# A 3x3 quantised convolution and a gated attention-free layer on one core: second layer in two TensorE visits a quarter instead of four

## The reference

```
# layer 0: x = x + L0(_gn(x))
v  = round(clip(x * in_factor, -1, 1) * 127) / 127 * 0.6, H and W swapped, padded by 1
fv = patches + 0.1 * patches ** 3                        # 3x3 patches of v
g  = g_pos - g_neg                                       # 3 planes of 128x128x3x3 weights
outs[i] = einsum('bctfyx,ocyx->btfo', fv, g[i])          # 3 convolutions
mem = adc(outs[2]) + adc(outs[0]) * 4 + adc(outs[1]) * 2 + adc(outs[2])
L0  = mem * out_factor + bias
# layer 1: x = x + L1(_gn(x)), with z = _gn(x) as 128 x 4096 per image
q, k, v = Wq z, Wk z, Wv z                               # 64 x 4096 each
num = exp(B) (exp(k) * v);  den = exp(B) exp(k)
L1  = Wm (q * num / den)
```

## Time and profile before

| | us |
|---|---|
| median of 3 runs | 1563.71 |
| the profiled execution | 1562.54 |
| its span in the trace | 1560.5 |
| PE busy | 1454.3 (93%) |
| DVE busy | 1393.6 (89%) |
| ACT busy | 1155.7 (74%) |
| POOL busy | 503.7 (32%) |

### The profile page before, as it was taken

How to read it: one execution, slowest core, us unless ns; L and a number is a source line. 1 busy time by engine, 2 the same in 40 slices (tenths; PEclk the granted TensorE clock), 3 DMA queues, 4 the chain that set the end, 5 groups by cost and what they waited for, 6 DMA issues and landing times.

```text
span 1560.5 us, 22719 instructions
## 1 busy us (share of the span) xinstructions
PE 1454.3 (93%) x7792; PEld 622.2 (40%) x7792; DVE 1393.6 (89%) x2182; ACT 1155.7 (74%) x1501; POOL 503.7 (32%) x506
## 2 busy tenths in 40 slices
PE   2599999999999999999999999999999999999985
PEld 1354434344443434444343443434344443434332
DVE  5869898998989899898989989898998989899767
ACT  4447778786877878787787878778786877875463
POOL 3111333232433333243333323333332433333312
PEclk9799999999999999999999999999999999999997
DMA  5011012313222231322223132222313222221222
GB/s 203 1 54 30 26 28 50 113 28 108 55 63 73 55 108 28 108 55 70 67 54 109 28 109 57 57 80 53 110 28 108 55 58 78 55 55 28 68 68 81
DMA packets 29173, 103.80 MB, mean 67 GB/s; under 512 B 4032, under 2 KB 4224, under 8 KB 29056
## 3 DMA queue, kind: packets, MB, share of 16 engines
q1 hardware_dynamic: 20416, 70.86, 12.3%
q0 software_dynamic: 8640, 31.46, 10.6%
HBM read 37.29 MB, written 33.55 MB: 45 GB/s over the span
## 4 chain that ended last, share of the span: by engine, by line
PE 74%; DVE 18%; issue 5%; POOL 1%; ACT 1%; DMA 1%; DVEq 0%; SPq 0%; POOLq 0%; ACTq 0%
PE A L486 14%; PE A L488 12%; PE A L487 12%; PE L L546 7%; PE B L486 7%; PE B L488 7%; PE B L487 7%; PE L L590 4%; PE L L577 3%; DVE duo L1068 1%; DVE uall L1150 1%; DVE A L1120 1%; DVE duo L1117 1%; DVE uall L1123 1%; DVE q L1040 1%
## 5 line engine op out<-in xcount | busy, mean ns | idle before, releaser
L486 PE MATMUL A<-T,WH 128*128 128x504 f16 (+1 forms) x1152 | 438.9, 381 | 1.0 <-ACT uall L780 1.0
L488 PE MATMUL A<-T,WL 128*128 128x504 f16 (+1 forms) x1152 | 437.3, 380 | 0.0
L487 PE MATMUL A<-T,WH 128*128 128x504 f16 (+1 forms) x1152 | 437.3, 380 | 0.0
L1436 POOL TENSOR_TENSOR T<-t,T 128x512 f16<-128x512 f32 x192 | 244.5, 1298 | 407.5 <-ACT T L702 407.5
L745 ACT ACTIVATE junk<-xr,shift 128x1024 f16<-128x1024 f32 x244 | 280.1, 1148 | 7.3 <-DVE xr L1153 0.7
L1410 POOL TENSOR_TENSOR zl<-z,zh 128x512 f16<-128x512 f32 x120 | 150.8, 1276 | 397.7 <-ACT zh L813 396.7
L486 PE MATMUL B<-T,WH 128*128 128x504 f16 (+1 forms) x576 | 221.4, 384 | 25.9 <-POOL T L1436 16.3
L488 PE MATMUL B<-T,WL 128*128 128x504 f16 (+1 forms) x576 | 220.7, 383 | 0.9 <-issue 0.9
L487 PE MATMUL B<-T,WH 128*128 128x504 f16 (+1 forms) x576 | 220.7, 383 | 0.0
L486 PEld LDWEIGHTS A<-T,WH 128*128 128x128 f16 x1152 | 115.1, 100 | 194.0 <-issue 81.3
L488 PEld LDWEIGHTS A<-T,WL 128*128 128x128 f16 x1152 | 112.7, 98 | 136.2
(11 more groups left out here) (174 smaller groups left out, 2462.5 us busy)
## 6 DMA issues: line engine op xcount, KB each, us to landing
xr<-in_x_dram SPq DMA_DIRECT2D x64, 512.0 KB, 5.8
out_dram<-xr SPq DMA_DIRECT2D x64, 512.0 KB, 2.7
xr<-shared POOLq DMA_DIRECT2D x60, 512.0 KB, 4.6
xr<-in_L_conv_g_pos_dram SPq DMA_DIRECT2D x3, 576.0 KB, 9.4
xr<-in_L_conv_g_neg_dram SPq DMA_DIRECT2D x3, 576.0 KB, 11.8
xr<-in_L_conv_Wm_dram SPq DMA_DIRECT2D x2, 32.0 KB, 9.2
xr<-in_L_conv_Wq_dram SPq DMA_DIRECT2D x1, 32.0 KB, 11.3
xr<-in_L_conv_Wk_dram SPq DMA_DIRECT2D x1, 32.0 KB, 11.1
```

What stands on the lines that cost most here:

```text
L486: nc.tensor.matmul(to, wh, th, start=fresh and y == 1, stop=False, skip_group_check=True)
L487: nc.tensor.matmul(to, wh, tl, start=False, stop=False, skip_group_check=True)
L488: done = nc.tensor.matmul(to, wl, th, start=False, stop=y == 2, skip_group_check=True)
L1436: last = nc.gpsimd.tensor_tensor(low, t32[:, pair, :, :, :].rearrange("p t e w -> p (t e w)"), high, ALU.subtract)
```

## The change

The four visits of a quarter become two. The first does the keys and values of quarter k and, right after them, the mix of quarter k-1; it waits for `o_ready` of k-1 first. The second does the queries and then the sums of quarter k. Queries and mix now write `low_pair`, the pair that the convolution's taps 2 and 4 use, so PE waits for `m2_copied` before such a visit, and the convolution's next step waits for `q_copied` or `evicted` (`others_read`, `second_read`). ACT gets one more instruction a quarter, `copy_queries`, a copy of the queries to SBUF behind `guess`. DVE keeps four instructions after the sums, now all in `ratio`: the numerator is first multiplied by the queries. The mix is cut into 8 matmuls of 64x64 weights and 256 columns, where it was 2 of 64x128 and 512. Each quarter's slots stand in tables (`KV_PE` and so on; numbers from 36 up mean the following phase); `TAIL` holds those of image 14. The slot tuples of the first layer are changed as well. In the head, the scale of x comes before the second weight difference on POOL, the third difference waits for `sums_made` 2, and the low rows of group 1 of image 0 are made by DVE (`head_rows_low`) instead of POOL. The diff, without blank lines:

```diff
-L2_PE = (1, 3, 6, 7)
-L2_ACT = (1, 3, 6, 8)
-L2_DVE = (2, 5, 6)
-L2_POOL = (6, 8)
-X_STATS = (1, 3, 4, 6)
-X_SPREAD = 7
-X_GROUP = 9
-X_MOMENTS = 9
-COMBINE = (21, 0)
-DOUBLE = (12, 33)
-RESIDUAL = (25, 7)
-BIAS = (17, 31)
-X1_STATS = (28, 30, 9, 13)
-X1_SPREAD = 13
+KV_PE = (21, 32, 39, 45)
+SUMS_PE = (22, 33, 40, 46)
+KV_ACT = (21, 32, 39, 45)
+MIX_ACT = (32, 40, 45, 57)
+SUMS_ACT = (23, 34, 41, 45)
+Z_ACT = (18, 25, 35, 41)
+KV_DVE = (22, 33, 40, 46)
+SUMS_DVE = (24, 35, 42, 49)
+Z_POOL = (18, 25, 35, 42)
+ADD_POOL = (35, 42, 49, 59)
+TAIL = {"KV_PE": (20, 26, 32, 36), "SUMS_PE": (22, 28, 34, 38), "MIX_PE": (26, 32, 36, 39),
+        "KV_ACT": (20, 26, 32, 36), "SUMS_ACT": (22, 28, 34, 43), "MIX_ACT": (26, 32, 36, 46), "Z_ACT": (18, 23, 29, 35),
+        "KV_DVE": (21, 27, 33, 36), "SUMS_DVE": (23, 29, 35, 44), "Z_POOL": (18, 23, 29, 35), "ADD_POOL": (27, 33, 37, 48)}
+X_STATS = (0, 2, 4, 6)
+X_SPREAD = 9
+X_GROUP = 14
+X_MOMENTS = 15
+COMBINE = (20, 0)
+DOUBLE = (17, 35)
+RESIDUAL = (23, 8)
+BIAS = (17, 32)
+X1_STATS = (26, 31, 8, 9)
+X1_SPREAD = 12
 X1_GROUP = 15
-LOW = (28, 33, 7, 11)
+LOW = (28, 33, 8, 11)
 X1_MOMENTS = 15
-LEVEL = (17, 19, 21, 24)
-QUANTISE = (18, 20, 23, 26)
-SQUARE = (19, 22, 24, 26)
-CUBIC = (21, 22, 27, 29)
-TRANSFORM = (26, 31, 2, 13)
-HIGH = (27, 32, 6, 14)
+LEVEL = (17, 19, 20, 24)
+QUANTISE = (18, 20, 21, 25)
+SQUARE = (19, 21, 24, 26)
+CUBIC = (20, 22, 27, 33)
+TRANSFORM = (26, 29, 3, 11)
+HIGH = (30, 32, 6, 14)
...
+        q32 = pieces[3]
...
+        STEADY = {"KV_PE": KV_PE, "SUMS_PE": SUMS_PE, "MIX_PE": KV_PE[1:] + (KV_PE[0] + SLOTS,),
+                  "KV_ACT": KV_ACT, "SUMS_ACT": SUMS_ACT, "MIX_ACT": MIX_ACT, "Z_ACT": Z_ACT,
+                  "KV_DVE": KV_DVE, "SUMS_DVE": SUMS_DVE, "Z_POOL": Z_POOL, "ADD_POOL": ADD_POOL}
...
+        def second(name, p, slot, images):
+            prev2, prev = images[:2]
+            last = B - 1 if isinstance(p, int) and p >= B - 1 else None
+            if prev2:
+                table = TAIL if last and p - 2 == B - 2 else STEADY
+                for k, at in enumerate(table[name]):
+                    if at == slot + SLOTS:
+                        return p - 2, 2, k
+            if prev and (images[2] or not last):
+                table = TAIL if last and p - 1 == B - 2 else STEADY
+                for k, at in enumerate(table[name]):
+                    if at == slot:
+                        return p - 1, 3, k
+            return None
...
+            def others_read(p, slots, images):
+                prev2, prev, cur, nxt = images
+                for slot in slots:
+                    if slot == X_GROUP and nxt:
+                        pe.wait_ge(gvar[0], nth(p + 1, 1, 0))
+                    if slot == X1_GROUP and prev:
+                        pe.wait_ge(gvar[1], nth(p - 1, 1, 0))
+                second_read(p, slots, images)
+            def second_read(p, slots, images):
+                for slot in slots:
+                    at = second("MIX_PE", p, slot, images)
+                    if at:
+                        pe.wait_ge(evicted, nth(at[0], NG, at[2]))
+                    at = second("SUMS_PE", p, slot, images)
+                    if at:
+                        pe.wait_ge(q_copied, nth(at[0], NG, at[2]))
...
-                    if n == X_GROUP // 6 + 1 and nxt:
-                        pe.wait_ge(gvar[0], nth(p + 1, 1, 0))
-                    if n == X1_GROUP // 6 + 1 and prev:
-                        pe.wait_ge(gvar[1], nth(p - 1, 1, 0))
+                    if n:
+                        others_read(p, range(6 * n - 6, 6 * n), images)
+                    elif prev:
+                        earlier = (not (isinstance(p, int) and p <= 2), prev2, True, True)
+                        others_read(p - 1, range(SLOTS - 6, SLOTS), earlier)
...
             def keys_values(image, k, w):
                 pe.wait_ge(zh_ready, nth(image, NG, k))
-                if not w and (k or not (isinstance(image, int) and image == 0)):
-
-                    pe.wait_ge(evicted, nth(image, NG, k - 1))
...
-            def queries(image, k, w):
-                pe.wait_ge(ratio_ready, nth(image, NG, k))
-                project(banks[w][0], 0, w, crossed=True).then_inc(q_ready, 1)
-            def mix(image, k, w):
-                pe.wait_ge(o_ready, nth(image, NG, k))
-                for h in range(2):
-                    half = slice(h * IC, (h + 1) * IC)
-                    last = nc.tensor.matmul(banks[w][h], wmf[half, :], rec[w][half, :], start=True, stop=True)
+            def queries():
+                project(low_pair[:, 0, :], 0, 0, crossed=True).then_inc(q_ready, 1)
+            def last_queries(k):
+                pe.wait_ge(last_ratio, k + 1)
+                project(banks[k][0], 0, k, crossed=True).then_inc(q_ready, 1)
+            def mix(w, out):
+                for part in range(2):
+                    at = slice(part * QUART, (part + 1) * QUART)
+                    for r in range(2):
+                        rows = slice(r * IC, (r + 1) * IC)
+                        for c in range(2):
+                            cols = slice(c * IC, (c + 1) * IC)
+                            last = nc.tensor.matmul(out[r][cols, at], wmf[rows, cols], rec[w][rows, at],
+                                                    start=True, stop=True)
                 last.then_inc(mix_ready, 1)
-            def second_layer(image, c):
-                k, at = divmod(c, CYCLE)
-                if at == L2_PE[0]:
-                    keys_values(image, k, 0)
-                if at == L2_PE[1]:
-                    numerator_denominator(image, k, 0)
-                if at == L2_PE[2]:
-                    queries(image, k, 0)
-                if at == L2_PE[3]:
-                    mix(image, k, 0)
+            def second_layer(p, slot, images):
+                n, place = divmod(slot, 6)
+                values, mixed, summed_up = (second(name, p, slot, images) for name in ("KV_PE", "MIX_PE", "SUMS_PE"))
+                if mixed or summed_up:
+                    assert not images[2] or 2 <= place < 5
+                    if images[2]:
+                        pe.wait_ge(m2_copied, nth(p, STEPS, n))
+                        others_read(p, range(6 * n, slot), images)
+                    elif slot == 0:
+                        pe.wait_ge(m2_copied, nth(p - 1, STEPS, STEPS - 1))
+                        others_read(p - 1, range(SLOTS - 6, SLOTS), (True, True, True, False))
+                    else:
+                        others_read(p, range(slot), images)
+                    if X_GROUP == slot and images[3]:
+                        pe.wait_ge(gvar[0], nth(p + 1, 1, 0))
+                    if X1_GROUP == slot and images[1]:
+                        pe.wait_ge(gvar[1], nth(p - 1, 1, 0))
+                if mixed:
+                    pe.wait_ge(o_ready, nth(mixed[0], NG, mixed[2]))
+                if values:
+                    keys_values(values[0], values[2], 0)
+                if mixed:
+                    mix(0, (low_pair[:, 0, :], low_pair[:, 1, :]))
+                if summed_up:
+                    queries()
+                    numerator_denominator(summed_up[0], summed_up[2], 0)
...
-                    if slot == 2 and not cur:
+                    if slot == 1 and not cur:
...
+            def copy_queries(image, k):
+                act.wait_ge(q_ready, nth(image, NG, k))
+                nc.scalar.copy(q32, low_pair[:, 0, :]).then_inc(q_copied, 1)
...
-                                     last_pair[:, :, :].rearrange("p c (r n) -> p c r n", r=2), ACT.Identity,
+                                     low_pair[:, :, :].rearrange("p c (r n) -> p c r n", r=2), ACT.Identity,
...
+            def second_layer(p, m, slot, images):
+
+                at = second("KV_ACT", p, slot, images)
+                if at:
+                    exponent(at[0], at[2], 0)
+                at = second("MIX_ACT", p, slot, images)
+                if at:
+                    evict(at[0], at[2])
+                at = second("SUMS_ACT", p, slot, images)
+                if at:
+                    guess(at[0], at[2], 0)
+                    copy_queries(at[0], at[2])
+                at = second("Z_ACT", p, slot, images)
+                if at:
+                    z_split(at[0], (m + at[1]) % RING, at[2])
...
+            def head_rows_low(g):
+                for pair in range(3):
+                    dve.wait_ge(th_ready, NP * g + pair + 1)
+                    high, low = (T[:, part, pair, g * TILES:(g + 1) * TILES, :, :]
+                                 .rearrange("p t e w -> p (t e w)") for part in range(2))
+                    last = nc.vector.tensor_tensor(low, t32[:, pair, :, :, :].rearrange("p t e w -> p (t e w)"),
+                                                   high, ALU.subtract)
+                last.then_inc(tl_ready, 1)
...
             def ratio(image, k, w):
+                dve.wait_ge(q_copied, nth(image, NG, k))
```

(55 more changed lines are left out.)

80 lines of the change are left out of this document (35 added, 45 removed).

## The result

The changed kernel takes 1546.22 us (median of 4 runs, 1544.50 to 1546.89) against 1563.28 (4 runs, 1562.73 to 1565.27): ratio 0.9889 [0.9877, 0.9901], 17.1 us less. Forecast were 1533 and a range of 1515 to 1556. Sign and range hold; the gain is little more than half of what was forecast.

The account below looks back on a forecast made before the run. PE was taken to bound the steady part. Fewer visits 15.6, the ratio's wait 22.5, new waits -15.4, head 6.5 and tail 1.8 made 31.0 us less: 1533, range 1515 to 1556.

Parts of the forecast that it names:

- Fewer visits: PE: each join saves 0.11 us, the mix's new shape 0.04; 1.04 us an image, 15.6 in all (bounds 2.4 to 22.2).
- Rival (C): PE: the shape change inside a joined visit costs 0.11 us, leaving 2.4 of 15.6 us; 1546, chance 0.05.
- (d): Ratio before keys, eviction before queries (0.8 us ahead at best), POOL's low rows, ACT's extra copy: no new wait.
- (c): DVE's weighted values of quarter 1 (slot 33) come about 0.2 us late for PE's sums.
- (b): ACT's m2 copy at first visits comes late for PE: 0.35 us at slot 9, about 0.25 at slot 32.
- (a): ACT's queries' copy at second visits, slots 22, 40, 46: PE stalls about 0.1 us each, 0.3 an image.
- (A): Waits move to where PE and ACT meet in `low_pair`, 2.4 us an image; 12.8 less, 1551, chance 0.13.
- (B): Slower: queries' copy 1.25 us late at three second visits, 4.55 us new waits an image; 1581, chance 0.10.
- (D): DVE becomes the bound; contention with POOL adds 1 us to its run, 14 us come back; 1547, chance 0.10.
- The signs: Image 88.6 to 89.8 us; over 1 us wait at slots 22, 40 or 46 proves (B), L577 wait on DVE's values (D).
- The head: Before the first convolution matmul: PE starts at about 42.2 instead of 49.55 us; 6.5 us gained (bounds 2.5 and 8).
- The tail: Last phases: 5.9 us of waits go, 0.4 and 3.7 are lost; 1.8 us gained (bounds -4 and +6).

Follow-up runs that it names:

- the last run: Changed kernel plus the edits for statistics order, sums at slot 34, doubling at slot 33, queries' copy ahead of Ln and Exp, and image 14's later mix: 1521.63 us.
- the run with fewer low rows: Changed kernel with two of POOL's three low-row subtractions of group 2 left out from the third image on: 1534.98 us.
- The statistics run: Changed kernel with ACT's last two statistics pairs and quarter 3's Ln, Exp and copy one slot later, so the eviction comes ahead: 1532.29 us.
- The tail run: Changed kernel with image 14's last mix behind the group sums of image 15, its eviction, ratio and addition moved with it: 1545.58 us.

## Why the prediction was right or wrong

- **Fewer visits: right, in mechanism and size.** Forecast 2.44 and 1.79 us for the joined visits, measured 2.44 and 1.80; an image without waits is 90.21 - 2.1 = 88.1, as forecast, and 88.46 with 0.3 of waits in the last run. The Trainium skill ("TensorEngine Tiling (Array Packing)", section Tiling Modes, Key Properties) says that changing the tiling mode drains TensorE, and the trace agrees: every change of shape shows 0.31 us between starts instead of 0.22, at the entry to a visit (722.79 to 723.10), in its middle (724.21 to 724.52) and at its end (725.22 to 725.54). Two visits apart have four such changes and a joined visit three. One of them was already in each piece's own time, because the prediction counted that to the start of the next matmul; so the change in the middle is there, and the price of a join, one change less, holds. Rival (C), a further 0.11 us in each joined visit, is out.
- **The ratio's wait goes: right.** No row of it is left in the steady part.
- **(d), taken at nothing: this is the term that was wrong.** The prediction says "`evicted` before the queries of the next slot: 0.8 us ahead at best" and took it at nothing, although it added that "a shift of 1 us uncovers" it. It measured 1.05 us an image, 14.7 us in 14; the three other terms together came out as they were forecast, 1.08 against 1.1. That agreement is partly luck: (c) came out larger, (a) and (b) smaller. The walk through ACT's list used undisturbed durations; the residual that the statistics wait for was 3.30 us long and not 2.35, and L1225 ahead of it 1.99 and not 1.23. That is 1.7 us, against 0.8 of slack (1.9 with the clipping ahead of both, L1222, at 0.91 instead of 0.69, which leaves 1.1); the run with fewer low rows took 0.95 of it away, and that left 0.10 of the wait. The statistics run ended it too, by the order alone. The prediction had a row of such a stretch, 3.52 against 1.22 us, and used it for the head only; with it the term would have been an interval, 0 to about 1 us, and not nothing.
- **(c), the weighted values: right mechanism, size off.** 0.2 forecast, 0.58 measured. DVE's run from the values of one quarter to the next took 28.8 us instead of 28.5; it also started a little late, behind a quantisation.
- **(b), the copy of m2: about half.** Slot 32 as forecast (0.25, measured 0.32); at slot 9, where 0.35 was forecast, 0.03 to 0.1.
- **(a), the copy of the queries: less** than forecast (0.3): 0.18 an image.
- **The rivals.** (A), "the new meeting point of PE and ACT in `low_pair`", named this mechanism with 2.4 us an image and 1551. The result, 2.1 us an image and 1546, is nearer to it than to the forecast of 1.1 and 1533, and the 0.13 that it got was too little for a walk with three meetings within 0.4 us. (B) did not happen: the copy was late by 0.06 at each of its three places, not 1.25. (D) named contention of POOL with DVE and its size, 1 us an image, but made DVE the bound; it acted through ACT, and in the last run PE is busy for 88.19 of 88.46 us and DVE for 84.88. (C) and (D) name 1546 and 1547, the time that was measured, by mechanisms that the trace does not show; that is chance.
- **The signs were too loose.** A wait of more than 1 us at slot 46 "would prove B", and a wait of the sums on DVE's values D. Both came: the first matmul at slot 46 waits up to 1.3 us, the sums 0.58 an image. But the first waits for the eviction and not for the queries' copy, and the second stayed at half a microsecond. A sign has to name the instruction that is waited for, and the size.
- **The head: nearly right.** First convolution matmul at 41.71 us (forecast 42.2), 7.84 earlier. 5.8 us of it are left at the group sums (forecast 6.5), because 2.0 us are lost on the way and not 0.7; of the waits for the weights on that way one is shown below (L1034, 3.73 us). Timeline of the head, against the earlier trace rows: the transform's first instruction is back at 1.22, as forecast, but POOL's second difference now lies beside the sums of plane 0, and one of these (L1018) takes 3.12 us, where it takes 0.84 later, with POOL idle:

```profile
16.83 3.15 POOL L1460 TENSOR_TENSOR xr<-xr 128x1152 f32<-128x1152 f32 x1 [0.22 <-DMA xr<-in_L_conv_g_neg_dram]
17.49 3.12 DVE L1018 SCALAR_TENSOR_TENSOR shared<-xr,shared 128x384 f32<-128x384 f32 x1
...
35.26 1.22 DVE L1132 TENSOR_TENSOR duo<-f 128x1024 f32<-128x1024 f32 x1 [1.75 <-POOL T L1521]
...
41.71 0.58 PE L504 MATMUL B<-T,WH 128*128 128x512 f16 x1 [11.45 <-DVE T L1158]
43.91 0.84 DVE L1018 SCALAR_TENSOR_TENSOR shared<-xr,shared 128x384 f32<-128x384 f32 x1
...
63.68 0.61 PE L504 MATMUL B<-T,WH 128*128 128x512 f16 x1 [3.73 <-DVE WL L1034]
```

- **The tail: about right in sum** (2.8 forecast with the joins of the last four quarters; 4.0 measured from the last phase's group sums on, 2.2 with what the odd images took back). The prediction's terms for its 3.7 lost add up to 3.6. The place named, the mix of quarter 3 and its eviction ahead of the group sums, is there (9.39 and 1.34 us of waits). The tail run shows that it costs less than it seems, since ACT and POOL make the last image's input no earlier.

## What to carry to other kernels

Where two engines meet in a shared buffer, look up what stands ahead of the releasing instruction on its engine, and what that in turn waits for: each of these may belong to another stage. Walk such a chain once with undisturbed durations and once with those of rows that lie beside a busy POOL; a slack smaller than the difference is an interval, not a nothing. When a stall is cured by delaying a consumer, follow what is queued behind the consumer's output: one slot more before the sums took 7.3 us of waits away and brought 8.9 back.

## What the runs showed of the hardware

In the rows read here, DVE instructions whose operands are all in SBUF and POOL's subtractions lengthen each other: 1.23 to 1.99 us (L1225), 2.35 to 3.30 (L1228) and 0.84 to 3.12 (L1018, 128x384, beside a 128x1152 subtraction) on DVE, and from 3.40 to 5.43 for three subtractions of one shape on POOL. With two of POOL's three left out, L1228 was back at 2.35. DVE's instructions with an operand in PSUM kept their time beside POOL's subtractions (L1195 takes 0.70 us at 728.11, where POOL subtracts nothing, and the same beside POOL's low rows):

```profile
745.04 3.52 POOL L1521 TENSOR_TENSOR T<-t,T 128x512 f16<-128x512 f32 x3 [5.00 <-ACT T L766]
746.54 0.70 DVE L1195 TENSOR_TENSOR A<-A,m 128x512 f32<-128x512 f32 x1
```

The Trainium skill ("GPSIMD Engine Reference", section 1, Specifications) states the contention for instructions with two SBUF inputs, as these three have; the rows agree, with the sizes above.

On PE each change between matmuls of 128x128, 128x64 and 64x64 weights put about 0.09 us between starts on top of the usual 0.22 (0.31 at 723.10, 724.52 and 725.54).
